# Attention heads: the first guess in two parts, two counts of the smallest tile on VectorE, a shorter move

## What is computed

```python
draft = jnp.einsum('bhqd,bhkd->bhqk', qr, kr)              # 32 heads, 1024 x 1024
draft = draft + jnp.where(causal_future, neg, 0.0)
_, draft_indices = jax.lax.top_k(draft, num_remain)        # num_remain = 128
mask = full(neg).at[..., draft_indices].set(0.0)
mask = jnp.where(causal_future, neg, mask)
scores = jnp.einsum('bhqd,bhkd->bhqk', qr, kr) / 4 + mask
attn = jax.nn.softmax(scores, axis=-1)
out = jnp.einsum('bhqk,bhkd->bhqd', attn, v)
```

## Time and profile before

| what | us |
|---|---|
| median of 3 runs | 3170.42 (3167.81 to 3173.41) |
| the profiled execution | 3171.23 |
| its span | 3169.4 |
| from the first guess (L2152) of head 0 to that of head 31 | 2073.3 to 2931.4 |
| from the cut of head 0 (L2199) to that of head 31 | 2127.1 to 3009.1 |
| one lap, from cut to cut | 28.63 |

### The profile page before, as it was taken

The page is one execution under the profiler, slowest core; times in us unless marked ns, Lnnn a source line. Parts: engine busy times, 40 slices in busy tenths (PEclk is TensorE's granted clock), DMA queues, the critical chain, the costliest instruction groups (busy, mean ns, idle before and its releaser), DMA issues. The chain is left out here.

```text
span 3169.4 us, 50416 instructions
## 1 busy us (share of the span) xinstructions
PE 2798.6 (88%) x15722; PEld 1527.9 (48%) x15833; DVE 2467.5 (78%) x4664; ACT 1952.2 (62%) x4186; POOL 1649.7 (52%) x3659
## 2 busy tenths in 40 slices
PE   8899999999999999999999989837777777777769
PEld 4455455455454464554554544514444444444444
DVE  5678687697696795786876977848999899998846
ACT  2464554564564554545545533569999999999823
POOL 3236245264263263362452544767777777777503
PEclk9999999999999999999999999958989899989889
DMA  2222122232232132231221320000000000000010
GB/s 90 66 80 94 70 97 80 73 107 70 77 116 84 63 104 80 77 103 67 90 90 60 100 75 1 28 1 2 2 2 2 2 2 2 2 2 2 1 51 27
DMA packets 65804, 169.62 MB, mean 54 GB/s; under 512 B 11776, under 2 KB 19328, under 8 KB 64512
## 3 DMA queue, kind: packets, MB, share of 16 engines
q1 hardware_dynamic: 54448, 115.17, 11.2%
q10 hardware_dynamic: 11088, 51.19, 4.6%
HBM read 161.08 MB, written 5.24 MB: 52 GB/s over the span
## 5 line engine op out<-in xcount | busy, mean ns | idle before, releaser
L2093 ACT ACTIVATE X<-ah_z,ah_trial 128x256 bf16<-128x256 f32 (+6 forms) x896 | 734.8, 829 | 51.4 <-POOL ah_trial L2194 41.9
L1207 ACT ACTIVATE m_mix<-m_mix,m_cs 128x128 f32<-128x128 f32 x1024 | 312.9, 388 | 253.6 <-DMA m_mix<-cs_rows 253.6
L1089 POOL TENSOR_TENSOR m_xdec<-m_xdt,m_decay_out 128x512 f32<-128x512 f32 x112 | 143.7, 1283 | 213.1 <-DVE m_xdt L1333 202.1
L2263 DVE TENSOR_SCALAR_CACHE_REDUCE X<-ah_z,ah_cut 128x256 bf16<-128x256 f32 (+6 forms) x224 | 193.7, 875 | 74.0 <-POOL ah_cut L2199 74.0
L1117 POOL TENSOR_TENSOR m_squares<-m_squares 128x256 f32<-128x256 f32 x128 | 108.3, 846 | 274.4 <-ACT m_squares L1219 274.4
L1013 PE MATMUL m_ps_d<-m_w_out,m_gate 128*128 128x512 f32 x512 | 235.2, 602 | 0.0
L1013 PE MATMUL m_ps_x<-m_w_out,m_gate 128*128 128x512 f32 x512 | 233.6, 599 | 0.0
L2104 ACT ACTIVATE X<-ah_ps_e 128x512 f32<-128x512 f32 (+3 forms) x384 | 185.7, 485 | 38.0 <-PE ah_ps_e L2015 27.8
L1975 PE MATMUL ah_ps_m<-a_kT,a_qT 128*128 128x512 bf16 (+3 forms) x318 | 106.2, 365 | 115.2 <-DVE tables L2292 114.7
L2284 DVE MAX8 ah_top<-ah_ps_m 128x8 f32<-128x256 f32 (+6 forms) x224 | 185.5, 828 | 22.6 <-PE ah_ps_m L1979 21.2
L2254 DVE TENSOR_SCALAR_CACHE_REDUCE ah_z<-ah_ps_z 128x256 f32<-128x256 f32 (+6 forms) x224 | 182.7, 816 | 15.9 <-PE ah_ps_z L1958 15.8
(11 more groups left out here) (326 smaller groups left out, 7483.2 us busy)
## 6 DMA issues: line engine op xcount, KB each, us to landing
m_mix<-cs_rows SPq DMA_DIRECT2D x128, 512.0 KB, 4.4
m_w_proj<-in_w_proj ACTq DMA_DIRECT2D x69, 512.0 KB, 3.3
m_fade<-fade_rows SPq DMA_DIRECT2D x224, 128.0 KB, 2.9
m_w_out<-in_w_out ACTq DMA_DIRECT2D x7, 2048.0 KB, 7.8
X<-in_x SPq DMA_DIRECT2D x8, 256.0 KB, 5.1
m_w_out<-in_w_out SPq DMA_DIRECT2D x1, 2048.0 KB, 10.0
x_away<-X SPq DMA_DIRECT2D x1, 2048.0 KB, 7.3
X<-x_away SPq DMA_DIRECT2D x8, 256.0 KB, 6.1
```

The costliest lines, as they stand in the source:

```text
L1207: act.activation(mix[:, u % 3, h, :], mix[:, u % 3, h, :], ACT.Relu, bias=cs[:, c, h0 + h:h0 + h + 1], scale=-1.0).then_inc(lag_done, 1)
L2093: act.activation(sign[:, at % 2, 0:(t + 1) * P], z[:, h % RING, cols(t)], ACT.Sign, bias=trial[:, h % RING, 0, t - 1:t], scale=-1.0, accum ...
L2263: dve.tensor_scalar(mark[:, (h * W + t) % 2, 0:(t + 1) * P], z[:, h % RING, cols(t)], cut[:, h % 2, t - 1:t], 0.0, ALU.is_ge, ALU.add, acc ...
```

## The change

There are three edits, all in `attention_heads_fast`.

First, the guess is split. `first_spread` holds the first six instructions (mean to standard deviation) and `first_cut` the other five (trial and bracket). GpSimd now runs `first_spread(n+1)` after the first move of lap n and `first_cut(n+1)` after the second.

Second, a move has one comparison less: the two comparisons "less than zero" become one that writes two slices of `side`. Some waits between its steps come later or earlier, and the product of bracket width and distance stands behind the power instead of between power and last product.

Third, in counts 0 and 2 the tile of 256 columns leaves ScalarE. VectorE counts the scores below the trial (`count_low`), with a sum that starts at -128; GpSimd doubles it into `signs` at the head of these moves. VectorE does count 2 of head n-1 at the start of lap n, ahead of the takes, and count 0 of head n+1 ahead of the pick of tile 4; the latter waits for `guessed` of head n+1.

```diff
+    ON_VECTOR = ((0, 0), (1, 2))
+    scalar_tiles = lambda k: range(2 if k in [q for _, q in ON_VECTOR] else 1, NT)
+    SCALAR_AT = {hkt: i for i, hkt in enumerate((h, k, t) for h, k in order for t in scalar_tiles(k))}
+    VECTOR_AT = {hk: i for i, hk in enumerate(hk for hk in order if hk[1] in [q for _, q in ON_VECTOR])}
...
             def count(h, k, t):
-                if t == 1 and k == 0:
-                    act.wait_ge(guessed, h + 1)
-                elif t == 1:
-                    act.wait_ge(moved, MOVE_AT[h, k - 1] + 1)
+                if t == scalar_tiles(k)[0]:
+                    if k == 0:
+                        act.wait_ge(guessed, h + 1)
+                    else:
+                        act.wait_ge(moved, MOVE_AT[h, k - 1] + 1)
...
-                        if live(n - back):
+                        if live(n - back) and t in scalar_tiles(k):
                             count(n - back, k, t)
...
                 pool.tensor_tensor(root, variance, env.half[:, 0:W], ALU.pow).then_inc(own, 1)
                 pool.wait_ge(own, at + 6)
+                steps[0] = at + 6
+
+            def first_cut(h):
+
+                at, r = steps[0], h % RING
                 pool.tensor_tensor(offset, root, table[:, 0], ALU.mult).then_inc(own, 1)
...
             def move(h, k):
-                pool.wait_ge(counted, (MOVE_AT[h, k] + 1) * W)
+                if (h, k) in VECTOR_AT:
+                    pool.wait_ge(counted_low, VECTOR_AT[h, k] + 1)
+                    pool.tensor_scalar(signs[:, r, 0:1], lower[:, r:r + 1], 2.0, None, ALU.mult).then_inc(own, 1)
+                    at += 1
+                    pool.wait_ge(own, at)
+                pool.wait_ge(counted, SCALAR_AT[h, k, NT - 1] + 1)
...
-                pool.tensor_scalar(side[:, 0], trial[:, r, 1], 0.0, None, ALU.is_lt).then_inc(own, 1)
+                pool.tensor_scalar(side[:, 0:3:2], trial[:, r, 1:2].to_broadcast([P, 2, W]), 0.0, None, ALU.is_lt).then_inc(own, 1)
                 pool.tensor_scalar(side[:, 1], trial[:, r, 1], 0.0, None, ALU.is_ge).then_inc(own, 1)
-                pool.tensor_scalar(side[:, 2], trial[:, r, 1], 0.0, None, ALU.is_lt).then_inc(own, 1)
...
+                pool.tensor_tensor(slope[:, 2], between[:, 0], toward[:, 1], ALU.mult).then_inc(own, 1)
                 pool.wait_ge(own, at + 13)
-                pool.tensor_tensor(slope[:, 1], between[:, 0], slope[:, 0], ALU.mult).then_inc(own, 1)
+                pool.tensor_tensor(slope[:, 1], slope[:, 2], slope[:, 0], ALU.mult).then_inc(own, 1)
                 pool.wait_ge(own, at + 14)
-                pool.tensor_tensor(slope[:, 2], slope[:, 1], toward[:, 1], ALU.mult).then_inc(own, 1)
-                pool.wait_ge(own, at + 15)
...
-                if live(n + 1):
-                    first_cut(n + 1)
-                for back, k in SWEEPS:
+                for slot, (back, k) in enumerate(SWEEPS):
                     if live(n - back):
                         move(n - back, k)
+                    if live(n + 1) and slot == 0:
+                        first_spread(n + 1)
+                    if live(n + 1) and slot == 1:
+                        first_cut(n + 1)
...
+            def count_low(h, k):
+                at = VECTOR_AT[h, k]
+                if k == 0:
+                    dve.wait_ge(guessed, h + 1)
+                    dve.wait_ge(z_done, h * NT + 2)
+                else:
+                    dve.wait_ge(moved, MOVE_AT[h, k - 1] + 1)
+                if at:
+                    dve.wait_ge(counted_low, at)
+                dve.tensor_scalar(below[:], z[:, h % RING, cols(1)], trial[:, h % RING, 0, 0:1], -float(P), ALU.is_lt, ALU.add,
+                                  accum_out=lower[:, h % RING:h % RING + 1]).then_inc(counted_low, 1)
...
+                if live(n - 1):
+                    count_low(n - 1, 2)
                 if live(n - 2):
                     take(n - 2, 1)
...
                 for t in range(1, NT):
+                    if t == 4 and live(n + 1):
+                        count_low(n + 1, 0)
```

More of the change, by code:

```diff
@@ L1870, in attention_heads_fast @@
         signs = sb("signs", [P, RING, W])
+        lower = sb("lower", [P, RING])
+        below = sb("below", [P, 2 * P], BF16)
         side = sb("side", [P, 3, W])
@@ L1908, in attention_heads_fast @@
             sem("s_done"), sem("z_done"), sem("sampled"), sem("stats_done"), sem("guessed"))
-        counted, moved, cut_done, own = sem("counted"), sem("moved"), sem("cut_done"), sem("own")
+        counted, counted_low = sem("counted"), sem("counted_low")
+        moved, cut_done, own = sem("moved"), sem("cut_done"), sem("own")
         take_done, marked, pick_step, pick_done, least_done = (
@@ L2133, in _, with first_spread @@
             mean, mean_square, squared_mean, reach, variance, root, offset = (guess[:, i] for i in range(7))
-            def first_cut(h):
+            def first_spread(h):
                 at, r = steps[0], h % RING
@@ L2156, in first_cut @@
                 pool.tensor_tensor(bracket[:, r, 1, 0], trial[:, r, 0], reach, ALU.add).then_inc(own, 1)
-                pool.wait_ge(own, at + 10)
-                steps[0] = at + 10
+                pool.wait_ge(own, at + 4)
+                steps[0] = at + 4
             def move(h, k):
                 at, r = steps[0], h % RING
-                pool.wait_ge(counted, (MOVE_AT[h, k] + 1) * W)
+                if (h, k) in VECTOR_AT:
[4 more added lines that the diff above has]
+                pool.wait_ge(counted, SCALAR_AT[h, k, NT - 1] + 1)
                 pool.tensor_tensor(trial[:, r, 1], signs[:, r], table[:, 2], ALU.subtract).then_inc(own, 1)
@@ L2176, in move @@
                 pool.tensor_scalar(missed[:, 0], trial[:, r, 1], 2.0 * (TOPK - LEAST), None, ALU.is_gt).then_inc(own, 1)
+                pool.wait_ge(own, at + 6)
+                pool.tensor_tensor(bracket[:, r], kept[:], moved_in[:], ALU.add).then_inc(own, 1)
                 pool.wait_ge(own, at + 7)
-                pool.tensor_tensor(bracket[:, r], kept[:], moved_in[:], ALU.add).then_inc(own, 1)
+                pool.tensor_tensor(missed[:, 1], missed[:, 0], side[:, 0], ALU.add).then_inc(own, 1)
                 pool.wait_ge(own, at + 8)
-                pool.tensor_tensor(missed[:, 1], missed[:, 0], side[:, 0], ALU.add).then_inc(own, 1)
+                pool.tensor_tensor(between[:], bracket[:, r, 1], bracket[:, r, 0], ALU.subtract).then_inc(own, 1)
                 pool.wait_ge(own, at + 9)
-                pool.tensor_tensor(between[:], bracket[:, r, 1], bracket[:, r, 0], ALU.subtract).then_inc(own, 1)
+                pool.tensor_tensor(toward[:, 1], toward[:, 0], missed[:, 1], ALU.mult).then_inc(own, 1)
                 pool.wait_ge(own, at + 10)
-                pool.tensor_tensor(toward[:, 1], toward[:, 0], missed[:, 1], ALU.mult).then_inc(own, 1)
+                pool.tensor_tensor(slope[:, 0], between[:, 1], table[:, 5], ALU.pow).then_inc(own, 1)
                 pool.wait_ge(own, at + 11)
-                pool.tensor_tensor(slope[:, 0], between[:, 1], table[:, 5], ALU.pow).then_inc(own, 1)
+                pool.tensor_tensor(slope[:, 2], between[:, 0], toward[:, 1], ALU.mult).then_inc(own, 1)
                 pool.wait_ge(own, at + 13)
-                pool.tensor_tensor(slope[:, 1], between[:, 0], slope[:, 0], ALU.mult).then_inc(own, 1)
+                pool.tensor_tensor(slope[:, 1], slope[:, 2], slope[:, 0], ALU.mult).then_inc(own, 1)
                 pool.wait_ge(own, at + 14)
-                pool.tensor_tensor(slope[:, 2], slope[:, 1], toward[:, 1], ALU.mult).then_inc(own, 1)
-                pool.wait_ge(own, at + 15)
-                steps[0] = at + 15
+                steps[0] = at + 14
                 if k < COUNTS - 1:
-                    pool.tensor_tensor(trial[:, r, 0], trial[:, r, 0], slope[:, 2], ALU.add).then_inc(moved, 1)
+                    pool.tensor_tensor(trial[:, r, 0], trial[:, r, 0], slope[:, 1], ALU.add).then_inc(moved, 1)
                     pool.wait_ge(moved, MOVE_AT[h, k] + 1)
@@ L2198, in move @@
                         pool.wait_ge(take_done, (h - 1) * W)
-                    pool.tensor_tensor(cut[:, h % 2], trial[:, r, 0], slope[:, 2], ALU.add).then_inc(cut_done, 1)
+                    pool.tensor_tensor(cut[:, h % 2], trial[:, r, 0], slope[:, 1], ALU.add).then_inc(cut_done, 1)
                     pool.sem_inc(moved, 1)
```

7 lines of the change are left out of this document (3 added, 4 removed).

## The result

| | before | after |
|---|---|---|
| median of the runs, us | 3170.43 | 3323.42 (3321.96 to 3325.86) |
| span of the profiled execution, us | 3169.4 | 3320.1 |
| cuts of head 0 and head 31, us | 2127.1, 3009.1 | 2120.4, 3160.2 |
| one lap in the middle of the heads, us | 28.63 | 34.13 |

The ratio is 1.0483, with a 95% interval of 1.0465 to 1.0501. The direction was forecast, the size was not: 3241 was predicted, and 3323 lies above the range of 3200 to 3281.

A forecast was written before the change was run, and what follows sets the result against it. ScalarE was taken as nearly full, VectorE close behind; a new 31.21 us loop replaces the 28.62 us lap: 29 laps by 2.59 is +75, opening -3.5, end -0.5, +71 in all: 3241 us, range 3200 to 3281.

The forecast's parts named there:

- The loop: Closed path of one lap through VectorE's added count, last evacuation, ScalarE's count, GpSimd's moves and guess: 31.21 us.
- the wait for the cut: VectorE's wait for GpSimd's cut, 74.0 us before, should fall to the opening one alone.
- that sign: ScalarE was to wait for VectorE's evacuations 3 us or more a lap, where it waited for moved trials before.
- that evacuation to ScalarE's count of the same tile, where ScalarE did wait for it: Loop step from VectorE's evacuation of 1024 columns to ScalarE's count of that tile: 1.27 us.
- GpSimd's stretch: Loop part from GpSimd's first move to the guess, two moves of 4.37 us, spread and doubling: 12.57 us.
- The upper end of the range: Longest lap, 32.6 us: moves stay at 4.68, count takes 0.5, one more marked-score wait follows VectorE's stop.
- The wait on the guess: VectorE's added count of the next head waits for GpSimd's guess about 3.3 us a lap, some 95 us.
- Rival 1: The guess is in time, so VectorE's own lap of 27.94 us decides: 3147 us; chance 0.06.
- Rival 2: No change: the loop exists but is 2.6 us a lap shorter than its rows, 28.6; chance 0.03.
- Rival 3: TensorE returns at 1.2 GHz after VectorE's stop, marked scores come late: 3280, up to 3300 us; chance 0.08.
- Rival 4: GpSimd's two-slice comparison costs as much as two, moves save nothing: +18 us, 3259; chance 0.83 shared with forecast.
- The rule on the most occupied engine: Relieve the engine of highest occupancy first, here ScalarE at 27.87 of 28.63 us; it would have made rival 1 the forecast.

The follow-up runs named there:

- e2_low_end: The changed kernel with VectorE's count 0 of the next head moved from ahead of pick 4 to the end of the lap, behind the last evacuation; 3130.0 us.
- e4_guess_early: The changed kernel with the whole guess in one piece ahead of GpSimd's first move again, both VectorE counts and the shorter move kept; 3169.9 us.

## Why the prediction was wrong in size

**The loop and its place: right. One link in it: wrong.** VectorE's added count waits for the guess in each lap, the wait for the cut is gone, the loop closes through the last evacuation, ScalarE and the first move, and every engine idles in it. But the prediction let ScalarE wait for VectorE's evacuations, 3 us or more a lap, and that sign did not come: from 1900 to 3210 us it does so 4 times in all, while it waits 237.6 us for TensorE's exponents. The way from evacuation to count leads through TensorE and an exponential.

```profile
ACT X L2101 <- DVE ah_z L2272: 4.9, 4, 1.3
```

**The term that failed** is "that evacuation to ScalarE's count of the same tile, where ScalarE did wait for it", 1.27 us. It was read in the earlier trace rows, in head 0, when no exponential was yet in ScalarE's queue. In the steady lap it is 4.01 us. The traces of before had it: in the lap already read for other terms, the evacuation began at 2437.06, and ScalarE's rows are

```profile
2439.66 0.49 ACT L2104 ACTIVATE X<-ah_ps_e 128x384 f32<-128x384 f32 x1
2440.04 1.03 ACT L2093 ACTIVATE X<-ah_z,ah_trial 128x896 bf16<-128x896 f32 x1
...
2441.07 1.14 ACT L2093 ACTIVATE X<-ah_z,ah_trial 128x1024 bf16<-128x1024 f32 x1
```

that is 4.01 us there too, with the same exponential ahead of the same two counts. In the kernel before the step takes 3.57 to 4.81 us in every head but the first. 29 laps of 34.13 - 31.21 = 2.92 us are 85 us, and 3241 + 85 = 3326, where 3323 was measured. Of the 2.92, 2.74 are this term, 0.25 GpSimd's stretch (moves of 4.50 us, not 4.37), -0.07 VectorE's. The upper end of the range, 32.6 us a lap, had no price for anything between evacuation and count.

**The wait on the guess** was forecast at 95 us and is 204, the same error seen from VectorE: its way from the evacuation of 1024 columns to the added count was forecast at 12.18 us and is 34.13 - 15.29 - 0.40 - 6.47 = 11.97; the guess's way was forecast at 15.45 and is 34.13 - 15.29 - 0.40 = 18.44.

**Rival 1** (the guess in time, 3147) has been built since, as e2_low_end: 3130. Its price took VectorE's lap as 27.94 us; with the same work the cuts there are 27.37 apart. The price had taken only the wait for the cut off the lap, though VectorE also stands 0.25 and 0.15 us for TensorE in it (at 2424.05 and 2426.10). **Rival 2** (no change) falls with the 153 us that the change costs. **Rival 3** (TensorE cold, marked scores late) falls: the granted clock did fall, from 0.88 and 0.94 to 0.85 in these laps, an average between its levels of 1.2 and 2.4 GHz, but VectorE's waits for marked scores fell from 21.2 us to 17.3, and its stretch from pick 4 to last evacuation did not grow. (Its price of 3280 lay inside the range, though its chance was counted outside.) **Rival 4** (the wider comparison saves nothing) falls too: the wide comparison takes 0.23 us to the next row (2600.37 to 2600.60), where one of seven columns took 0.21. Of 0.31 us taken off a move, 0.18 came: the product behind the comparisons now begins 0.33 us after the last of them (2600.60 to 2600.93), where it was 0.20.

**The rule on the most occupied engine**, which the prediction quoted from the Trainium skill, "Perfetto Trace Analysis", section "Identifying the Most-Contended Engine", gave the wrong sign for this change, and in e4_guess_early no gain at all, since relieving ScalarE in sweeps outside its loop only made it wait. It held once the loop was opened: after the split, ScalarE's 0.49 us were worth 17 us.

## What to carry to other kernels

Before an instruction of a busy engine is made to wait for a later result, follow the path from that engine's own output back to this wait over one whole turn; if it closes, its length is the new lap, and moving the waiting instruction to behind the last output that the path needs can open it. Read each step of such a loop in the steady lap and in the engine's queue order: what stands ahead of the step in the queue counts with all that it waits for. And before work is taken from the fullest engine, see whether that work lies in the loop that sets the lap; here two counts outside it brought nothing while the guess stood in it.

## What the runs showed of the hardware

For these small instructions GpSimd's price is per instruction, hardly per column: the doubling of one column takes 0.25 us and 0.33 to the next dependent step (2607.43 to 2607.76), as much as a comparison of seven columns or a sum of 28, 0.24 each. The power of seven columns is the exception, 1.51 us. So a small extra step on its path can use up what two saved steps elsewhere give, as in e4_guess_early.
